# Four pieces of VectorE's work moved to GpSimd and ScalarE or dropped, and gate, statistics and half a scaling moved ahead, in a gated attention and expert block

## The reference

```python
x = x + tanh(g_xattn[0]) * xattn(layernorm(x), ctx, ...)
x = x + tanh(g_ffn[0]) * ffn(layernorm(x), gate_W, gate_b, expert_W, expert_b)

def xattn(x, y, ...):
    q, k, v = x @ Wq + bq, y @ Wk + bk, y @ Wv + bv      # 16 heads of 16
    attn = softmax(q @ k.T / 4)
    h = relu((attn @ v) @ W1 + b1)                       # 512 wide
    return h @ W2 + b2

def ffn(x, gate_W, gate_b, expert_W, expert_b):
    p = softmax(maximum(x @ gate_W + gate_b, 1e-4))      # 8 experts
    top = top_k(p, 2)
    w = maximum(p, 0.1) / (sum of maximum(p, 0.1) over top)
    return sum over top of w * (x @ expert_W + expert_b) / 2
```

## Time and profile before

| | |
|---|---|
| median of 3 runs | 1005.38 us (1005.3 to 1008.52) |
| the profiled execution: its time, its span | 1003.91 us, 1002.2 us |
| busy share of the span | PE 94%, PEld 67%, DVE 83%, ACT 73%, POOL 65% |
| PE busy from 400 to 500 us | 98.08 of 100 us |

### The profile page before, as it was taken

One profiled execution on the slowest core, in us unless ns is written; L12 is line 12 of the kernel. 1 busy time (PEld: TensorE's weight loads), 2 busy tenths in 40 slices (PEclk: granted clock), 3 DMA queues, 4 the chain that ended last, 5 costly groups with the idle time before them and its releaser, 6 DMA issues.

```text
span 1002.2 us, 26189 instructions
## 1 busy us (share of the span) xinstructions
PE 941.7 (94%) x9410; PEld 668.3 (67%) x9410; DVE 834.1 (83%) x2137; ACT 732.1 (73%) x1517; POOL 650.5 (65%) x856
## 2 busy tenths in 40 slices
PE   3669999999999999999999999999999999999997
PEld 2446766766766776776777676677667766776753
DVE  5777888888888888888888889888888888888875
ACT  4756878777787877778787777778777877877661
POOL 5435766667776666776666677666677766666743
PEclk8589999999999999999999999999999999999999
DMA  6000000000000000000000000000000000000000
GB/s 196 27 14 11 15 14 25 25 25 22 26 14 15 25 26 25 23 23 17 15 25 25 25 23 14 26 15 25 25 25 22 15 17 23 25 12 12 12 13 22
DMA packets 17473, 24.62 MB, mean 25 GB/s; under 512 B 2799, under 2 KB 8897, under 8 KB 17345
## 3 DMA queue, kind: packets, MB, share of 16 engines
q1 hardware_dynamic: 17344, 22.94, 7.3%
HBM read 14.54 MB, written 8.39 MB: 23 GB/s over the span
## 4 chain that ended last, share of the span: by engine, by line
PE 56%; POOL 16%; DVE 9%; issue 9%; ACT 7%; DMA 1%; SPq 1%; POOLq 0%; DVEq 0%; ACTq 0%
PE e L735 19%; PE g L735 11%; PE t L918 9%; POOL k_block L427 8%; POOL p_lo L373 6%; PE t L784 4%; ACT p_hi L558 2%; PE g L935 2%; DVE stats L1086 2%; PE s L869 2%; DVE acc L1199 2%; PE s L804 1%; DVE kz L1252 1%; PE g L744 1%; DVE p_lo L1182 1%
## 5 line engine op out<-in xcount | busy, mean ns | idle before, releaser
L373 POOL TENSOR_TENSOR p_lo<-p_f,p_hi 77x512 f16<-77x512 f32 x160 | 183.4, 1162 | 227.6 <-ACT p_hi L558 227.6
L735 PE MATMUL e<-we_hi,x2T_lo 128*128 128x512 f16 x496 | 189.7, 382 | 4.8 <-DVE acc L1199 4.8
L735 PE MATMUL e<-we_hi,x2T_hi 128*128 128x512 f16 x496 | 188.9, 381 | 0.0
L735 PE MATMUL e<-we_lo,x2T_hi 128*128 128x512 f16 x496 | 188.9, 381 | 0.0
L557 ACT ACTIVATE p_f<-t 77x512 f32<-77x512 f32 x256 | 154.3, 603 | 24.2 <-PE t L784 23.8
L1199 DVE SCALAR_TENSOR_TENSOR acc<-e,comb,acc 128x256 f32<-128x256 f32 x307 | 146.0, 475 | 13.5 <-PE e L735 11.1
L558 ACT ACTIVATE p_hi<-t 77x512 f16<-77x512 f32 x256 | 154.4, 603 | 0.0
L1244 DVE TENSOR_REDUCE row_max<-s 128x6 f32<-128x462 f32 (+1 forms) x192 | 108.3, 578 | 32.1 <-PE s L869 32.0
L804 PEld LDWEIGHTS s<-v_hi,p_lo 77*128 77x128 f16 x1024 | 83.4, 96 | 38.3 <-issue 22.2
L804 PE MATMUL s<-v_hi,p_lo 77*128 77x17 f16 x1024 | 97.9, 172 | 11.0 <-DVE p_lo L1182 4.1
L806 PE MATMUL s<-v_hi,p_hi 77*128 77x17 f16 x1024 | 96.4, 170 | 0.0
(11 more groups left out here) (193 smaller groups left out, 2900.3 us busy)
## 6 DMA issues: line engine op xcount, KB each, us to landing
x_sb<-in_x SPq DMA_DIRECT2D x32, 256.0 KB, 2.6
out<-acc SPq DMA_DIRECT2D x32, 256.0 KB, 2.0
we_f<-in_L_ffn_expert_W SPq DMA_DIRECT2D x2, 1024.0 KB, 11.0
y_sb<-in_ctx SPq DMA_DIRECT2D x32, 57.8 KB
w_f<-in_L_xattn_W SPq DMA_DIRECT2D x2, 512.0 KB, 7.3
wq_f<-in_L_xattn_Wq SPq DMA_DIRECT2D x1, 256.0 KB, 3.9
wkv_f<-in_L_xattn_Wk SPq DMA_DIRECT2D x1, 192.0 KB, 3.1
wkv_f<-in_L_xattn_Wv SPq DMA_DIRECT2D x1, 192.0 KB, 3.9
```

The lines of the kernel that those rows point to most:

```text
L373: pool.tensor_tensor(p_lo[:, r].rearrange("m h n -> m (h n)"), p_f[:, r, :], p_hi[:, r].rearrange("m h n -> m (h n)"), ALU.subtract).then_ ...
L735: mm = pe.matmul(out_ap, a, c, start=(i == 0), stop=(i == n - 1))
```

## The change

- `h_low` of c = 1 and 3 goes from VectorE to GpSimd, ahead of and behind `v_parts`; the semaphore `h_lo_done` becomes one for each engine.
- `p_low` of pair 2 goes from VectorE to GpSimd.
- VectorE's half of `kz_copy` goes to ScalarE, which now makes both halves one after the other.
- The gate's second instruction (`gs`, a maximum with EPS) is dropped: a ninth column that holds EPS enters the row maximum, and the third instruction takes the maximum with EPS itself. 12 instructions are left.
- `gate 1` moves ahead of `yT_low`; the next five move together ahead of `kv_with_bias`, since `p_low(m, 2)` no longer stands between them; `gate 9` (10 before) stays behind `q_with_bias`.
- `first_norm_stats` moves ahead of `take_max(b, 2)`.
- The first half of `scale_expert` 3 moves ahead of `qs_copy_a` and `qs_copy_b` on ScalarE.
- On GpSimd `x_with_bias` moves behind `second_norm_scale`.

```diff
-POOL_LOW = (1, 3, 4, 5, 6)
-VECTOR_LOW = (0, 2, 7)
+POOL_LOW = (1, 2, 3, 4, 5, 6)
+VECTOR_LOW = (0, 7)
...
+            def h_low(b, c):
+                pool.wait_ge(relu_done, 8 * b + 2 * c + 2)
+                at_least(pool, mlp_in_psum, 2 * b)
+                pool.tensor_tensor(h_lo[:, c, :], h_f[:, c, :], h_hi[:, c, :].bitcast(F32), ALU.subtract).then_inc(h_lo_pool, 1)
...
                     q_low(b)
+                if has(s, -1):
+                    h_low(m, 1)
+                if has(s, 0):
                     v_parts(b, u)
+                if has(s, -1):
+                    h_low(m, 3)
...
-                if has(s, 1):
-                    x_with_bias(n, nu)
                 if has(s, -1):
                     second_norm_scale(m, 0)
                     second_norm_scale(m, 1)
+                if has(s, 1):
+                    x_with_bias(n, nu)
...
-                act.activation(kz[0:SLOT, :, 0, :], src[0:SLOT], ACT.Copy).then_inc(kz_done, 1)
+                for i in range(2):
+                    rows = slice(i * SLOT, (i + 1) * SLOT)
+                    act.activation(kz[rows, :, i, :], src[rows], ACT.Copy).then_inc(kz_done, 1)
...
+                if first:
+                    scale_expert(e, eu, 3, s - 2, (0,))
                 if front:
                     qs_copy_a(b)
                     qs_copy_b(b)
                 if first:
-                    scale_expert(e, eu, 3, s - 2)
+                    scale_expert(e, eu, 3, s - 2, (1,))
...
-                            pe.wait_ge(h_lo_done, 4 * b + c + 1)
+                            pe.wait_ge((h_lo_vector, h_lo_pool)[c % 2], 2 * b + c // 2 + 1)
...
                 elif k == 2:
-                    ins = dve.tensor_scalar(gs[:], graw[:], EPS, None, ALU.max)
+                    ins = dve.tensor_reduce(gm1[:], graw[:], AX.X, ALU.max)
                 elif k == 3:
-                    ins = dve.tensor_reduce(gm1[:], gs[:], AX.X, ALU.max)
+                    ins = dve.scalar_tensor_tensor(out=gshift[:], in0=graw[:, :, 0:E], scalar=EPS, in1=wide(gm1),
+                                                   op0=ALU.max, op1=ALU.subtract)
...
                 if front:
                     take_max(b, 1)
-                    take_max(b, 2)
-                    kz_copy(b)
                 if has(s, 1) and s > 0:
                     first_norm_stats(n_pair, n, nu)
+                if front:
+                    take_max(b, 2)
```

More of the change, by code:

```diff
@@ L632, in scale_expert @@
                 at_least(act, scaled_added, 2 * b)
-                for j in range(2):
+                for j in parts:
                     act.activation(scaled[:, j, t, :], BANK[product_banks(r)[i]][:, j * D:(j + 1) * D], ACT.Copy,
@@ L1276, in h_low @@
                     at_least(dve, mlp_in_psum, 2 * b)
-                dve.tensor_tensor(h_lo[:, c, :], h_f[:, c, :], h_hi[:, c, :].bitcast(F32), ALU.subtract).then_inc(h_lo_done, 1)
+                dve.tensor_tensor(h_lo[:, c, :], h_f[:, c, :], h_hi[:, c, :].bitcast(F32), ALU.subtract).then_inc(h_lo_vector, 1)
             def add_mlp(b, u, t):
@@ L1329, in gate @@
                 elif k == 5:
-                    ins = dve.tensor_tensor(gdiff[:], gs[:].unsqueeze(2).to_broadcast([P, T, E, E]),
-                                            gs[:].unsqueeze(3).to_broadcast([P, T, E, E]), ALU.subtract)
+                    ins = dve.tensor_tensor(gbeat[:], gdiff[:], beat_from[:], ALU.is_gt)
                 elif k == 6:
-                    ins = dve.tensor_tensor(gbeat[:], gdiff[:], beat_from[:], ALU.is_gt)
+                    ins = dve.tensor_reduce(gcount[:], gbeat[:], AX.X, ALU.add)
@@ L1334, in gate @@
                 elif k == 7:
-                    ins = dve.tensor_reduce(gcount[:], gbeat[:], AX.X, ALU.add)
+                    ins = dve.tensor_reduce(gsum[:], gexp[:], AX.X, ALU.add)
                 elif k == 8:
-                    ins = dve.tensor_reduce(gsum[:], gexp[:], AX.X, ALU.add)
-                elif k == 9:
                     ins = dve.scalar_tensor_tensor(out=gfloor[:], in0=wide(gsum), scalar=W_THRES, in1=gexp[:],
                                                    op0=ALU.mult, op1=ALU.max)
-                elif k == 10:
+                elif k == 9:
@@ L1367, in step @@
                     p_low(m, 0)
+                if first:
+                    gate(e, eu, 1)
                 if front:
@@ L1374, in step @@
                 if first:
-                    gate(e, eu, 1)
                     gate(e, eu, 2)
                     gate(e, eu, 3)
+                if first:
                     gate(e, eu, 4)
-                if mid:
-                    p_low(m, 2)
-                if first:
                     gate(e, eu, 5)
                     gate(e, eu, 6)
-                    gate(e, eu, 7)
                 if front:
@@ L1389, in step @@
                 if first:
+                    gate(e, eu, 7)
                     gate(e, eu, 8)
-                    gate(e, eu, 9)
                 if front:
@@ L1394, in step @@
                 if first:
-                    gate(e, eu, 10)
+                    gate(e, eu, 9)
                 if front:
@@ L1406, in step @@
                 if first:
-                    gate(e, eu, 11)
+                    gate(e, eu, 10)
                 if last:
@@ L1410, in step @@
                 if first:
-                    gate(e, eu, 12)
+                    gate(e, eu, 11)
                 if last:
@@ L1414, in step @@
                 if first:
-                    gate(e, eu, 13)
+                    gate(e, eu, 12)
                 if last:
@@ L1456, in step @@
                     h_low(m, 0)
-                    h_low(m, 1)
                 if first:
@@ L1463, in step @@
                     add_expert(e_pair, e, eu, 1, 1, s - 2)
-                if mid:
-                    h_low(m, 3)
                 if front:
```

35 lines of the change are left out of this document (17 added, 18 removed).

## The result

The changed kernel takes 1052.96 us in the median of 4 runs (1052.52 to 1057.72), the kernel before 1005.51 us in the runs beside it: a ratio of 1.047, 95% interval 1.044 to 1.050. It is slower, as forecast, but by 47 us and not by 5, far outside the range of 1000 to 1018 us.

A forecast was written before the change was run, and what follows sets the result against it. TensorE, busy 98 of 100 us, was taken as the bound, mlp_down's end hanging on mlp_up, ReLUs and h_lo. -0.26 + 0.30 + 0.14 = +0.18 us a step, 5.2 us over 29 steps: 1010.5 us, range 1000 to 1018.

The forecast's parts named there:

- The step that failed: GpSimd, idle 1.74 us from 428.56 to 430.30: p_lo 2 of 1.16 fits there and p_lo 5's chain is not delayed.
- rival C: GpSimd's p_lo 2 and 3 hold up gdiff and gbeat, making kv_with_bias late: +0.44 a step, 1018 us; chance 0.16.
- The front: Step's start on ScalarE: with half a scaling moved ahead, xnT_hi, p_lo 0 and attend 0 come 0.26 us sooner.
- The length of h_lo on GpSimd: End of mlp_down: GpSimd's h_lo takes 0.71 and h_lo 3 ends at 447.57, not 447.26; loss 0.30 a step.
- xn2 loses against xb: Second norm: VectorE's xn2 waits for GpSimd's xb, delaying TensorE's x2 transposes; 0.14 us a step, bounds 0 and 0.20.
- rival B: Second norm: xn2 gets in before xb, no loss there; +0.04 a step, 1006.6 us; chance 0.26.
- Rival D: h_lo 3 on GpSimd costs hardly anything, xn2 isn't held up, front's 0.26 stays; -0.24 a step, 998.4 us; chance 0.16.
- The second kz copy: ScalarE: it lies in the wait for mlp_up and costs nothing; were that too short, all ReLUs late by the overrun.
- The wait ahead of expert 2: TensorE's 0.17 us wait for VectorE's acc goes, but mlp_down's c = 3 takes it back: nothing gained.

The follow-up runs named there:

- 7: Kernel before with only the half scaling ahead and the gate's first operation ahead with its floor dropped: 998.5 us.
- 6: Changed kernel with p_lo 2, h_lo of chunks 1 and 3 and x_with_bias back in their old places: 1002.1 us.
- 10: Changed kernel with p_lo of pair 2 and h_lo of chunks 1 and 3 back on VectorE: 1010.0 us.
- run 1: Changed kernel with p_lo of pair 2 back on VectorE, between the gate's third and fourth operation: 1016.1 us.
- Run 11: Changed kernel with two ScalarE copies exchanged, qhT before khT: 1024.0 us.
- run 9: Kernel before with h_lo of chunks 1 and 3 on GpSimd alone: 1018.6 us.
- run 8: Kernel before with x_with_bias behind both second_norm_scale pieces alone: 1009.2 us.
- run 3: Changed kernel with h_lo of chunks 1 and 3 back on VectorE in their old places: 1046.5 us.
- run 4: Changed kernel with a wait added: GpSimd's first key_blocks instruction waits until VectorE's p_lo of pair 7 has ended: 1028.7 us.
- run 5: Kernel before with one needless instruction of 0.19 us on GpSimd ahead of its p_lo of pair 6 in each step: 1060.0 us.
- run 12: Run 7 with the wait of run 4 in its second and third step alone: 994.7 us.
- 2: Kernel before with p_lo of pair 2 on GpSimd alone, its place on VectorE empty: 1064.0 us.

## Why the prediction was wrong

The runs give each part its price by the table's steps, one after another, as each was added to the one before it:

| part | forecast a step | measured a step | from runs |
|---|---|---|---|
| half scaling ahead, shorter gate | -0.26 | -0.27 | before, 7 |
| kz on ScalarE, statistics ahead | 0 | +0.13 | 7, 6 |
| x_with_bias behind the second norm | +0.14 | +0.21 | 6, 10 |
| h_lo 1 and 3 on GpSimd | +0.30 | +0.30 | 10, 1 |
| p_lo 2 on GpSimd, with the turn kept | 0 | +0.28 | 1, 11 |
| the turn | 0 | +1.01 | 11, changed |
| sum | +0.18 | +1.66 | |

Run 11 also exchanges two copies, which makes k_block later (TensorE waits up to 0.5 for it, 0.2 before), so the 0.28 holds that too, and the 1.01 is at least what the turn costs.

**The step that failed** is one paragraph: p_low of pair 2 "fits, and the long chain ... is not delayed". I compared its 1.16 us with GpSimd's idle 1.74 and took idle time for room. For GpSimd's own queue it was room: p_lo 3 and 4 start 5.77 and 7.16 us into the step, and 5.77 and 7.17 in run 1. But it was the time in which gdiff and gbeat ran. Through them kv_with_bias, the copy of the keys and exps 5 come late, so that p_lo 5 starts at 9.49 in place of run 1's 9.15 and p_lo 6 ends 0.34 later, while khT is only 0.23 later. The forecast saw the first half of this as rival C, where it stood with 0.16 and a delay of about 0.4 in a price of 0.44 a step. C's conditions were met to the letter (gdiff and gbeat 1.2 and 1.3 long, kv_with_bias 0.81 later), and with the turn kept p_lo 2 measures 0.28. The second half, in which that shift of a tenth at the end of p_lo 6 hands VectorE's turn to k_block, no case held: I looked for what p_lo 2 does to instructions beside it, and not for who comes next at the places further on where VectorE waits for GpSimd.

That could have been asked of the trace of before. There VectorE's p_lo of pair 7 ends 0.55 behind GpSimd's, and k_block behind it, already released, is 0.45 longer than it need be: two instructions wanted the ports, and khT was 0.12 ahead, a tenth short of the 0.22 from which the runs show the other outcome. The same trace holds a lost turn, too: in its second step, with khT 0.70 ahead, VectorE's p_lo of pair 7 takes 4.46.

**What was right.** The front, from ScalarE's queue, to 0.01. The length of h_lo on GpSimd, 0.72 for 0.71, from v_lo's row, the place of the last one (run 9), and its price. That xn2 loses against xb (0.06 behind is enough), so rival B is out; its price was 0.21 and not 0.14, and alone it is nothing (run 8), so it is no cost of the move but of the move together with the half scaling. Rival D is out with h_lo at 0.72.

**What was too cheap.** The second kz copy: "in ScalarE's wait for mlp_up" holds only up to 0.57 of its 0.70, the overrun that the forecast named as the price and set to nothing. The wait ahead of expert 2, said to vanish, is 0.3 long in the changed kernel and in run 3, and it is gone in run 1 and, but for a single one of 0.2, in runs 4 and 11: where the turn is lost, VectorE's acc comes late again.

Open is what sets TensorE's clock in the first three steps, and with it most of the third step's length, 30.6 to 34.8 us in these kernels. TensorE was busy 0.94 of the 3 us from 66 to 69 us in the kernel before, 0.97 in run 6 and 0.41 in run 8, at a clock of 1.00 in all three; then it stayed at 1.00 until 81 us in the first and fell to 0.50 by 72 us in the other two.

## What to carry to other kernels

Idle time of GpSimd beside a busy VectorE is not room: look at which VectorE instructions with two SBUF inputs, and which tensor_scalars, run in it, and price the move by what they lose. Then go on to every later place where a VectorE instruction already waits for GpSimd, and see what GpSimd has queued behind, and how early that is released; a tiny shift there decides over a whole instruction (0.19 us of work cost 54 us). Where VectorE's piece is the urgent one, give it the turn on purpose: a wait for it in GpSimd's queue, or a later release of the next GpSimd instruction, was worth 24 to 29 us here.

## What the runs showed of the hardware that was not expected

- **Asking first does not win.** In run 5 VectorE's p_lo asks at 459.40, and k_block is released only at 459.54, 0.14 later; in the kernel before it is 435.29 and 435.42, 0.13 later. Yet k_block goes first in the one and p_lo in the other. What differs is how long before the end of GpSimd's p_lo 6 the release comes, 0.26 and 0.12. There are 401 such places in the traces of the 13 kernels other than run 4, without the two steps in which run 12's wait decides. VectorE went next in all 272 where khT was ready at most 0.223 us ahead of that end, and GpSimd in all 129 where it was ready at least 0.225 ahead, whether VectorE had asked up to 0.16 ahead of khT or up to 0.17 behind it. Two third steps stand close on either side: run 8's, shown there, with 0.228, and that of the kernel before with 0.220 (GpSimd's p_lo ends at 81.49):

```profile
80.95 0.32 ACT L588 ACTIVATE khT<-g 128x154 f16<-128x154 f16 x1
81.12 0.92 DVE L1182 TENSOR_TENSOR p_lo<-p_f,p_hi 77x512 f16<-77x512 f32 x1 [0.70 <-ACT p_hi L558]
81.45 1.70 POOL L427 TENSOR_TENSOR k_block<-own_head,khT 128x616 f16<-128x616 f16 x1
```

The Trainium skill (SBUF — State Buffer, Who interferes with whom) says that issue order decides who blocks, and that whoever issues first gets the shared pair for a whole instruction. That agrees with gbeat, 0.01 behind p_lo 3, and with xn2, 0.06 behind xb, which both stood to the end. It does not settle these rows, where VectorE had asked first both times; read as a rule for the next turn, it would have let p_lo go next in both, and run 5 would not have lost it. The measurement decides: GpSimd kept the ports for its next instruction wherever that was released early enough, four in a row in run 7's second step.

- **A release that comes sooner can cost.** Exchanging two copies so that khT comes 0.5 us later made the kernel 28.9 us faster.
- **One lost turn draws a second.** In runs 2 and 5 the step lost 0.9 us at attend 7 and then 0.6 to 0.7 at mlp_down, since what came late met a GpSimd instruction that had kept its time.
